# A two-layer graph network on one core: the order of VectorE's and TensorE's work in the edge loops

## The reference

```python
# layer 0, per edge e = (src, dst), sh = (es, ev) of edge_attr_4, r of edge_attr_16
out_s = (x_s[src] * es) @ W_ss  +  (x_v[src] . ev) @ W_vv
out_v = (x_s[src] x ev) @ W_sv  +  (x_v[src] * es) @ W_vs
msg   = [out_s, out_v] * sigmoid(r @ W_rad.T + b_rad)
h     = x + segment_sum(msg, dst);  x = layernorm(x + linear(h))

# layer 1, per edge; f0, f1 are linear features of the nodes
w     = silu(r @ Wfc1) @ Wfc2            # 192 radial weights
mid   = products of w, f0[src], f1[src] and sh   # 384 columns
n     = segment_mean(mid, dst);  x = layernorm(x + f(n, x))
```

## Time and profile before

| | |
|---|---|
| median of 3 runs | 5723.65 us (5711.29 to 5736.86) |
| the profiled execution | 5735.73 us, span 5733.9 us |
| mean granted TensorE clock | 0.699 of full speed |
| edge loop of layer 0 | about 90 to 2727 us of the span |
| edge loop of layer 1 | about 2838 to 5655 us |

### The profile page before, as it was taken

The page is one execution under the profiler, slowest core; times in us unless marked ns, Lnnn a source line. Parts: engine busy times, 40 slices in busy tenths (PEclk is TensorE's granted clock), DMA queues, the critical chain, the costliest instruction groups (busy, mean ns, idle before and its releaser), DMA issues.

```text
span 5733.9 us, 82997 instructions
## 1 busy us (share of the span) xinstructions
PE 3993.3 (70%) x16478; PEld 2635.1 (46%) x16479; DVE 3889.5 (68%) x12732; ACT 3382.4 (59%) x10841; POOL 3141.9 (55%) x3275
## 2 busy tenths in 40 slices
PE   5656565656566566666777777777777777777877
PEld 4445454545455455545544443444444344444435
DVE  4676777777777767777566666666666666666667
ACT  4666666666666666666555555555555555555555
POOL 4555555555555555555355555555555555555551
PEclk7555555555555555555888888888888888888888
DMA  7555555555555555555222222222222222222221
GB/s 239 150 147 154 148 152 148 152 148 154 146 150 152 148 151 148 151 149 133 79 76 76 75 74 74 73 75 74 75 73 74 76 76 78 75 74 76 77 76 51
DMA packets 325631, 641.98 MB, mean 112 GB/s; under 512 B 143598, under 2 KB 175131, under 8 KB 325499
## 3 DMA queue, kind: packets, MB, share of 16 engines
q0 software_dynamic: 181584, 557.89, 35.6%
q1 hardware_dynamic: 144016, 83.72, 5.6%
HBM read 620.47 MB, written 20.88 MB: 112 GB/s over the span
## 4 chain that ended last, share of the span: by engine, by line
PE 34%; DVE 28%; another core or an unknown queue 16%; issue 12%; ACT 6%; DVEq 3%; DMA 1%; ACTq 0%; POOL 0%; SPq 0%
PE ps L907 22%; DVE work L625 9%; DVE onehot L660 5%; ACT work L433 5%; DVE work L609 5%; PE ps L900 4%; PE ps L883 3%; PE ps L892 3%; DVE arena L632 1%; DVE work L612 1%; DVEq L676 1%; DVE work L648 1%; DVEq L721 1%; PE ps L870 1%
## 5 line engine op out<-in xcount | busy, mean ns | idle before, releaser
L361 POOL DMA_INDIRECT work<-table,srcs x1616 | 1559.9, 965 | 1237.8 <-issue 511.1
L361 POOL DMA_INDIRECT arena<-table,srcs x1616 | 1537.2, 951 | 1137.8 <-DVE work L609 619.3
L433 ACT ACTIVATE work<-arena,dst_sh 128x96 f32<-128x96 f32 (+1 forms) x4848 | 1415.7, 379 | 430.8 <-DVE arena L632 379.2
L907 PE MATMUL ps<-work,onehot 128*128 128x384 f32 x3616 | 1535.0, 578 | 180.6 <-DVE work L655 129.8
L433 ACT ACTIVATE work<-work,dst_sh 128x96 f32<-128x96 f32 (+1 forms) x4848 | 1499.6, 398 | 23.6 <-issue 10.8
L883 PE MATMUL ps<-wrad,escal 17*128 17x160 f32 x3232 | 561.2, 494 | 1033.9 <-DVE arena L632 857.5
L907 PEld LDWEIGHTS ps<-work,onehot 128*128 128x128 f32 x3616 | 771.3, 223 | 854.7 <-issue 524.7
L907 PE MATMUL ps<-arena,onehot 128*128 128x161 f32 x3616 | 1082.8, 479 | 12.3 <-issue 9.2
L907 PEld LDWEIGHTS ps<-arena,onehot 128*128 128x128 f32 x3616 | 925.0, 320 | 140.6 <-issue 131.2
L883 PEld LDWEIGHTS ps<-wrad,escal 17*128 17x128 f32 x3232 | 405.7, 309 | 1189.8 <-issue 840.6
L517 ACT ACTIVATE hid<-ps 128x256 f32<-128x256 f32 x404 | 152.0, 376 | 1180.6 <-remote 924.6
(11 more groups left out here) (122 smaller groups left out, 2057.7 us busy)
## 6 DMA issues: line engine op xcount, KB each, us to landing
escal<-in_escal SPq DMA_DIRECT2D x404, 98.0 KB
arena<-table,srcs POOLq DMA_INDIRECT x1616
work<-table,srcs POOLq DMA_INDIRECT x1616
table<-work SPq DMA_DIRECT2D x49, 224.0 KB, 2.6
dst_sh<-in_dst_sh SPq DMA_DIRECT2D x404, 20.0 KB
table<-work SPq DMA_DIRECT2D x7, 784.0 KB, 4.0
acc<-in_xd SPq DMA_DIRECT2D x1, 3920.0 KB
arena<-in_xd SPq DMA_DIRECT2D x7, 560.0 KB, 4.1
```

Of the source, the lines that this page charges most:

```text
L361: pool.indirect_dma_start(out=rows[:, j, t, :], out_offset=None, in_=table, in_offset=bass.IndirectOffsetOnAxis(ap=srcs[:, b, j, t:t + 1], ...
L433: last = nc.scalar.activation(u[:, t, to:to + c1 - c0], r[:, t, c0:c1], ACT.Copy, scale=dst_sh[:, j, at:at + 1].bitcast(f32))
L907: last = mm(bank(to)[:, 0:(MSG0, MSG1)[l]], onehot[:, b, t, :], m[:, j % 2, t, :], start=t == 0, stop=t == TPS - 1)
```

## The change

On VectorE, `weight_by_one` moves ahead of the wait for finished sums and their addition. What were the first instructions of the message functions, the two part sums of layer 0 and the first part sum of layer 1, become functions of their own (`parts0`, `parts1`) and move ahead of that wait too, directly behind the weighting. One-hots and the rest of the messages stay behind the addition. On TensorE the radial product of layer 0 moves behind the sums of the same supertile, and the wait for the messages that stood before it is dropped, since `windows` waits for the same count. Layer 1 keeps its order on TensorE. No instruction with data is added or taken away.

```diff
-            def messages0(s, j):
-
-                u, m, c = weighted0[:, j % DEEP0, :, :], msg0[:, j % 2, :, :], rad[j % 2]
+            def parts0(s, j):
+
+                u = weighted0[:, j % DEEP0, :, :]
                 dve.wait_ge(s_wone[0], s + 1)
                 dve.wait_ge(s_wtd[0], s + 1)
...
                 summed(u[:, :, 0:MS], 160, 3)
                 summed(u[:, :, MS:2 * MS], 224, 2)
+
+            def messages0(s, j):
+
+                u, m, c = weighted0[:, j % DEEP0, :, :], msg0[:, j % 2, :, :], rad[j % 2]
                 dve.wait_ge(s_part[0], s * 2 + 2)
                 dve.wait_ge(s_act[0], s + 1)
                 nc.vector.tensor_tensor(m[:, :, 0:DIM], u[:, :, 0:DIM], c, ALU.mult).then_inc(s_msg[0], 1)
 
+            def parts1(s, j):
+
+                u = weighted1[:, j % 2, :, :]
+                dve.wait_ge(s_wone[1], s + 1)
+                dve.wait_ge(s_wtd[1], s + 1)
+                nc.vector.tensor_tensor(half[:, :, 0, 0:MV], u[:, :, 224:256], u[:, :, 416:448], ALU.add).then_inc(s_part[1], 1)
+
             def messages1(s, j):
...
-                dve.wait_ge(s_wone[1], s + 1)
-                dve.wait_ge(s_wtd[1], s + 1)
-
-                nc.vector.tensor_tensor(h[:, :, 0, 0:MV], u[:, :, 224:256], u[:, :, 416:448], ALU.add).then_inc(s_part[1], 1)
                 dve.wait_ge(s_w2, s + 1)
...
                 def supertile(s, i, j, window, more):
                     dve.wait_ge(s_dsh[l][j // PAIR], (i + 1) * 16)
                     nc.vector.tensor_copy(dstf[:, j % 2, :], dst_sh[:, j, 0:TPS]).then_inc(s_dstf[l], 1)
+                    weight_by_one(l, s, i, j)
+                    (parts0, parts1)[l](s, j)
                     dve.wait_ge(s_agg[l], s + 1)
                     dve.wait_ge(s_add[l], s + 1)
                     add_sums(l, FIRST + j % 2, held(waiting)).then_inc(s_add[l], 1)
-                    weight_by_one(l, s, i, j)
                     dve.wait_ge(s_dstf[l], s + 1)
                     select(j, j % 2, window).then_inc(s_oh[l], 1)
                     (messages0, messages1)[l](s, j)
...
                 def supertile(s, i, j, more, left=SUPS):
 
-                    if l == 0:
-                        if left > 2:
-                            pe.wait_ge(s_msg[0], s + 1)
-                            radial0(s + 2, i + (j + 2) // SLOTS, (j + 2) % SLOTS)
-                    else:
+                    if l == 1:
                         if left > 1:
                             radial1(s + 1, (j + 1) % SLOTS)
                         if left > 2:
                             hidden1(s + 2, i + (j + 2) // SLOTS, (j + 2) % SLOTS)
                     windows(l, s, i, j, more, visit)
+                    if l == 0 and left > 2:
+                        radial0(s + 2, i + (j + 2) // SLOTS, (j + 2) % SLOTS)
```

## The result

The changed kernel takes 5912.69 us (median of 4 runs, 5901.9 to 5922.37); the kernel before, run beside it, 5717.47 us (median of 4, 5707.64 to 5736.86). The ratio is 1.033, 95% interval 1.0308 to 1.0353: slower by 3.3%. The profiled execution took 5901.9 us, its span is 5900.1.

What follows compares the result with a forecast made beforehand. Late TensorE signals and POOL's 5.0 us of gathers per supertile were taken as the bound. 117 us saved in layer 0 plus 17 in layer 1 gave 134 less, so 5590 us against the 5723.65 median; range 5300 to 5860.

Steps and rivals of the forecast that it cites:

- slower rival: Both layers, second rival: a gather more before each wait lengthens it; layer 0 loses 121 us, total 5893; chance 0.26.
- runs of four and five: Layer 0: four or five supertiles from one late-signal release to the next, 6.24 us per supertile instead of 6.53.
- 4.3 us of tolerance: Layer 0: second sums after a release end at R + 8.9 and are needed at R + 13.2.
- break-even of 3.6: Layer 0: supertiles per run at which the change neither gains nor loses, from 5.5 / n = 1.53.
- the forecast's 117: Layer 0: us saved by VectorE's reordering, (6.53 - 6.24) x 404 supertiles.
- R + 3.9: Layer 0: POOL issues its next gather 3.9 us after a release R of the waiting add, against 2.0 before.
- TensorE's part at nothing: Layer 0: radial product behind the sums makes the sigmoid 0.4 us late, priced at 0; bounds 0 and 483.9 us.
- SP at nothing: Load of dst_sh 0.4 us late, 202 times, at most 81 us; priced at 0 because ScalarE has a supertile's slack.
- 17 us saved: Layer 1, VectorE: 85 us gained from hoisted weighting and first part sum, less 68 lost behind waits for ScalarE.
- 95 us of its worst end: Layer 1: nothing saved and each second one of the 191 add waits grows by 1 us.
- The late signals do not lengthen with the gathers: First rival: runs hardly ever break, 396 us saved in layer 0, 40 in layer 1, total 5288; chance 0.22.
- The signs it named: Profile after: fewer add waits; POOL's L609 wait below 300 us means first rival, POOL standing over 700 us the second.

Runs made afterwards that it cites:

- h2: VectorE's part of the change alone, both layers, TensorE's order as before, against the kernel before: 5923.05 us, ratio 1.0328.
- n2: Only the weighting moved ahead of the addition, both layers, part sums behind the one-hots, TensorE as before, against the kernel before: 5961.69 us, ratio 1.0404.
- n1: h2 plus a wait on POOL that holds the gathers of supertile s+4 until the add of s: 5616.48 us, 0.9802 of the kernel before.
- o1: Full change plus a wait on POOL holding the gathers of s+4 until the add of s: 5873.68 us, 1.0087 of the kernel before (5825.27).
- i: Layer 0's two TensorE signals carried late by SyncE's small DMAs: order of before 4806.88 us, full change 4587.62; kernel before 4393.09.
- k: As i, with DMAs of 128 pieces and dst_sh loaded earlier: order of before 6365.13 us, VectorE's part 6165.04, full change 6053.20; kernel before 5732.95.
- f1: Full change once more, on a chip where signals come on time: 4393.7 us against 4391.31 for the kernel before, ratio 1.0009.

## Why the prediction was wrong

The forecast was 5590 us and the range ended at 5860; measured were 5912.69. The slower rival, "one more gather before each wait", gave 5893 us, and it is the one whose mechanism the runs bear out.

**What bounds the kernel.** Right: POOL's 5.0 us per supertile plus its pauses, and late signals that "often come only once POOL has stopped". The runs made that remark the likeliest cause of the loss: let the gathers go ahead and it comes (h2, n2), hold them and it is gone (n1).

**VectorE, layer 0: the step that failed is "I take runs of four and five, 6.24 us".** It gave the second sums "4.3 us of tolerance for a signal that is 3 to 8 us late". The tolerance was reckoned against the lateness of *before*, though the text had just let four more gathers go ahead of the signal, and with these out the signals came up to 15.0 us late (h2). After the change the runs hold 2.73 supertiles in the mean, and of 146 that lie whole in layer 0 106 have exactly three: below the break-even of 3.6 which the prediction itself had worked out. Its sum for a run of three was 6.83 us per supertile; 2702.6 / 404 = 6.69 were measured. The sum would have given 7.0 for runs of 2.73; the pause of a run was put too long in it, 5.5 us, where 4.51 were measured. The evidence it set against the rival, that "the mean of the 194 waits is 3.33", was the wrong row: a mean of waits with gathers up to s+3 says nothing of those with s+4.

**The value of the hoist itself.** With the gather held back, layer 0 gains 139 us (2628 to 2489, n1), if one takes the kernels before of the two jobs, 5736 and 5729 us, as equal. So the work hidden under the wait is a real gain, and the side effect through POOL takes 225 us away (2489 to 2714, h2, again in two jobs). That 139 lies near the forecast's 117 is chance: 117 was reckoned for gathers let go early, with a restart at R + 3.9 and runs of four and five, while n1 restarts at R + 1.1 in the release shown and has runs of 2.66.

**Restart and release.** R + 3.9 for POOL's next gather and 2.86 us from its last issue to the release were forecast; the release of h2 shown above has 4.9 and 3.8, and over all its late add signals the release comes 2.7 us after the last issue in the middle.

**TensorE's part at nothing.** Right as a sum, as far as was measured: 0.9998 and 1.0004 with signals on time; and where they are late, 1.033 for the full change and 1.0328 without TensorE's part, in two jobs. TensorE's order alone was never run there, and o1 leaves open that it costs something once the gathers are held. The text's clause, "if it goes, it goes with the late signals", is what the profile after shows (L636 behind L459, 429.6 us), but it costs nothing more: VectorE waits 744 us for the add and hardly at all for the message product in layer 0 of h2, 125 and 515 us in that of the kernel after. Under carried signals the same move gained 148 us.

**SP at nothing.** Right for the change: ScalarE waits 3.8 us for dst_sh in layer 0 of the kernel after. With VectorE's part alone it waits 104.7 us (h2), more than the 81 of the range, and 128.8 in n1, which is faster all the same.

**Layer 1: "17 us saved", 90 lost.** The 95 us of its worst end was the better number. The part sum's wait was named and came, but at 305.9 us, not "well over 67.6"; ScalarE's hidden product waits 208 us more. With the gathers held (n1) layer 1 is 91 of h2's 106 us shorter. So here too it was the gather, not the part sum behind ScalarE, for that wait stays (283.9 us in n1).

**The rivals.** "The late signals do not lengthen with the gathers" is what i and k built, and there the change gained as that rival said. On the real signals it is refuted by n1 and n2.

**The signs it named.** The add's waits became fewer and were no shorter than 3.3 us, as the forecast wanted. But POOL's wait for L609 fell from 619.3 to 99.9 us, below the 300 that were to speak for the first rival, and that was misleading: POOL now waited 438.4 us for ScalarE's weighting instead. The second rival's sign came in kind, waits of the sigmoid and of L636 in place of the add's, with POOL's pauses at 663 us in place of 563, short of the 700 named. A sign should be put on all that an engine waits for, not on one releaser.

## What to carry to other kernels

Work moved ahead of a wait also gives its *own* signals earlier. Before counting what it hides, list who waits for those signals and what they will start, and ask whether that can delay the very signal being waited for; if so, keep the release where it was (here one semaphore wait on POOL, worth 5% between h2 and n1; measured in two jobs, and with n1 at two runs). And a lateness read from a trace belongs to the order of that trace: it is not a constant to set a new order's slack against.

## What the runs showed of the hardware that was not expected

The same kernel takes 4390 to 4396 us in five jobs, 5717 to 5733 in three and 5825 in one, and each stays within 0.6% inside its job. One chip number appears with both 4391 and 5729 us, so it is open whether this is the chip or what else its host does. At 4.39 ms the trace has the semaphore's event within 0.03 us of the recorded end for all 404 sums and all 404 radial products of layer 0 (f1), with more gathers per us in flight. At 5.7 ms (the kernel before) it has one within 0.2 us for only 74 sums and 65 radial products; the others come later or are missing from the trace, and the latest radial product of h2 that was waited for came 17.2 us behind its recorded end.

Where POOL stood, the signals came near the end of the last gather's own traffic. The DMA packets of a gather end 3.1 us after its issue (median at long pauses, before, h2 and n1 alike), and the add's signals came in the middle 0.4 us ahead of that end in the kernel before, 0.2 us behind it in h2 and 0.1 us behind it in n1. Some came 2 us and more ahead of it. What holds them was not found. The ends of TensorE's records are modelled, so the trace doesn't tell a late signal from a late last result; TensorE did start its next work meanwhile, as the sums at 1619.01 in the earlier trace rows stand ahead of the release at 1625.15.

TensorE's granted clock over layer 1 is 0.84 of full speed in the kernel after, whose stretch has 2184 us of its recorded work in 2898 us, and 0.97 in f1, with 1895 us in 2060.
